# First sweep of a two-layer graph network: quads of slots instead of pairs on TensorE and ScalarE, gathered rows copied two quads ahead

## The reference, cut to what matters

```python
h = relu(layernorm(x))
x_l, x_r = h @ W_l + b_l, h @ W_r + b_r
e_emb = ea @ W_e                                    # ea: 64 features of each edge
m = leaky_relu(x_l[src] + x_r[dst] + e_emb, 0.2)
alpha = einsum('ehf,hf->eh', m, att)                # one score for each edge and head
ex = exp(alpha - segment_max(alpha, dst)[dst])
out = segment_sum(x_l[src] * (ex / denom[dst])[..., None], dst)   # self loops take part
x = x + relu(batchnorm(out.mean(heads) + bias))
```

## Time and profile before

| | before |
|---|---|
| median of three runs | 6867.18 us (6836.62 to 6873.22) |
| span of the profiled execution | 6810.8 us |
| PE busy | 4219.0 us |
| POOL busy | 3619.4 us |
| DVE busy | 3344.2 us |
| ACT busy | 1439.7 us |

### The profile page before, as it was taken

The page is one execution under the profiler, slowest core; times in us unless marked ns, Lnnn a source line. Parts: engine busy times, 40 slices in busy tenths (PEclk is TensorE's granted clock), DMA queues, the critical chain, the costliest instruction groups (busy, mean ns, idle before and its releaser), DMA issues. The chain is left out here.

```text
span 6810.8 us, 81310 instructions
## 1 busy us (share of the span) xinstructions
PE 4219.0 (62%) x16760; PEld 3105.7 (46%) x16761; DVE 3344.2 (49%) x8382; ACT 1439.7 (21%) x6145; POOL 3619.4 (53%) x3589
## 2 busy tenths in 40 slices
PE   4777777777777777768999998533333333333335
PEld 3555555555555555644444445333333333333335
DVE  6444444444444444479999998822222222222224
ACT  1111111111111111236666663400000000000000
POOL 2555555555555555305555551056666666666662
PEclk8888888888888888879999998755555555555555
DMA  6333333333333333324343441201111111111111
GB/s 106 92 93 95 93 93 94 95 99 95 96 93 93 98 92 93 98 81 124 110 111 109 110 112 50 57 20 23 23 23 23 23 23 23 23 23 23 23 23 28
DMA packets 609795, 478.35 MB, mean 70 GB/s; under 512 B 424696, under 2 KB 438034, under 8 KB 609334
## 3 DMA queue, kind: packets, MB, share of 16 engines
q1 hardware_dynamic: 440940, 256.05, 14.3%
q0 software_dynamic: 101184, 104.41, 7.2%
q10 hardware_dynamic: 67465, 115.81, 4.7%
HBM read 348.37 MB, written 126.73 MB: 70 GB/s over the span
## 5 line engine op out<-in xcount | busy, mean ns | idle before, releaser
L1417 POOL DMA_INDIRECT BR<-h2D,mS x1564 | 1476.9, 944 | 1007.4 <-issue 451.5
L585 POOL DMA_INDIRECT BR<-hD,AL x1308 | 1247.2, 953 | 1018.4 <-ACT ZR L634 638.4
L1441 PE MATMUL PS<-BR,ZR 128*128 x3328 | 796.1, 426 | 1507.1 <-DVE ZR L544 1086.3
L616 PE MATMUL PS<-Wz,BR 128*128 128x264 f32 x3328 | 1209.0, 449 | 696.3 <-DVE alq L682 319.0
L1441 PEld LDWEIGHTS PS<-BR,ZR 128*128 128x128 f32 x3328 | 735.9, 328 | 1567.3 <-issue 1563.9
L679 DVE SCALAR_TENSOR_TENSOR PS<-PS,a 128x528 f32<-128x528 f32 x832 | 594.8, 715 | 1543.4 <-PE PS L617 653.6
L1460 DVE TENSOR_TENSOR BR<-BR,PS 128x64 f32 x1664 | 362.6, 218 | 1725.3 <-remote 1306.5
L617 PE MATMUL PS<-BR 128*128 x3328 | 1150.8, 431 | 0.0
L940 PE MATMUL PS<-BR,ZR 128*128 128x329 f32 x3328 | 1027.9, 469 | 27.0 <-POOL BR L926 21.0
L616 PEld LDWEIGHTS PS<-Wz,BR 128*128 128x128 f32 x3328 | 653.9, 219 | 839.0 <-issue 587.1
L926 POOL TENSOR_TENSOR BR<-ZR,BR 128x768 f32<-128x768 f32 x416 | 616.1, 1481 | 416.6 <-ACT BR L912 414.7
(11 more groups left out here) (254 smaller groups left out, 2641.4 us busy)
## 6 DMA issues: line engine op xcount, KB each, us to landing
zD<-ZR ACTq DMA_DIRECT2D x416, 256.0 KB
ZR<-zD SPq DMA_DIRECT2D x416, 256.0 KB, 2.7
BR<-relD SPq DMA_DIRECT2D x105, 512.0 KB
ZR<-ea SPq DMA_DIRECT2D x1664, 32.0 KB
BR<-h2D,mS POOLq DMA_INDIRECT x1564
BR<-hD,AL POOLq DMA_INDIRECT x1308
AL<-hD SPq DMA_DIRECT2D x28, 224.0 KB, 2.6
BR<-hD,lmS POOLq DMA_INDIRECT x256
```

The lines of the kernel that those rows point to most:

```text
L585: Q.indirect_dma_start(HT[:, (t % G) * F:(t % G) * F + F], None, hD, bass.IndirectOffsetOnAxis(at_src, 0)).then_inc(hs[q % 16], 16)
L616: P.matmul(m, zo1[:, p % 2, (j % 2) * 128:(j % 2) * 128 + 128], Wz, start=True, stop=False)
L1417: Q.indirect_dma_start(BIG[:, j * F:j * F + F], None, h2D, bass.IndirectOffsetOnAxis(mS[:, (j // 16) % 4, j % 16:j % 16 + 1], 0)).then_inc ...
L1441: ins = P.matmul(bank3(j // 4)[:, j % 4, :], oh[:, (j // 4) % 4, j % 4, :], rows, start=True, stop=True)
```

## The change

In the first sweep, TensorE turns four slots into one whole PSUM bank and signals once; ScalarE copies 512 columns at once and signals once; TensorE takes that once for the two pairs of products. The quad q+1 is turned before the products of quad q. ScalarE copies the gathered rows of quad q+2 while it handles quad q, and two quads ahead of the loop. Its order for a quad is: copy of the turned quad, the register load where it is due, four row copies, the store. `zo1` becomes two buffers of 512 columns, of which the second lies beyond the old end of the tensor. To make room, `Wzs` (weights that are needed only after the sweeps) moves into the big tensor, is stored to DRAM before the sweep and loaded again after it. The register tables `ringD` and `needD` are shifted by the added quad.

```diff
-    BR = sb("BR", [128, 26000 + NS * 4 + 16 * AC])
+    BR = sb("BR", [128, 26000 + NS * 4 + 16 * AC + MC])
-    Wzs = sb("Wzs", [128, MC])
+    Wzs = BR[:, 26000 + NS * 4 + 16 * AC:26000 + NS * 4 + 16 * AC + MC]
-    zo1 = Rf[:, 1408:1920].rearrange("p (t c) -> p t c", c=256)
+    zo1 = Rf[:, 1408:1920], BR[:, 26000 + NS * 4 + 4992:26000 + NS * 4 + 5504]
+    wzsD = dram("wzsD", [128, MC])
...
+    dWs = dsem()
+    sv.wait(S)
+    dma(S, wzsD, Wzs, dWs)
...
+    dWs.wait(A)
...
-            def turn(p):
-                for j in (2 * p, 2 * p + 1):
-                    if j % 4 == 0:
-                        hc.take(P)
-                        es[(j // 4) % 8].take(P, 64)
-                    ins = P.transpose(PS[:, p % 2, (j % 2) * 128:(j % 2) * 128 + 128],
-                                      zring[:, j % 32, :, :].rearrange("p t f -> p (t f)"), ident)
+            def turn(q):
+                hc.take(P)
+                es[q % 8].take(P, 64)
+                for k in range(4):
+                    ins = P.transpose(PS[:, q % 2, k * 128:k * 128 + 128],
+                                      zring[:, (4 * q + k) % 32, :, :].rearrange("p t f -> p (t f)"), ident)
                 ins.then_inc(t_rdy.s, 1)
...
-                zo_rdy.take(P)
+                if p % 2 == 0:
+                    zo_rdy.take(P)
...
             turn(0)
-            for p in range(32):
-                if p + 1 < 32:
-                    turn(p + 1)
-                products(p)
+            for q in range(16):
+                if q + 1 < 16:
+                    turn(q + 1)
+                products(2 * q)
+                products(2 * q + 1)
...
+        def rows_of_quad(q, regs):
+            gf.take(A)
+            A.wait_ge(landed, regs[1])
+            for k in range(4):
+                ins = source_row(regs[0][k], 4 * q + k)
+                if k == 0:
+                    ins.then_inc(hf.s, 1)
+            ins.then_inc(hc.s, 1)
...
-            for p in range(32):
-                q = p // 2
+            for q in range(16):
                 t_rdy.take(A)
-                A.copy(zo1[:, p % 2, :], PS[:, p % 2, 0:256]).then_inc(zo_rdy.s, 1)
-                if not (last and q == 15):
-                    if p % 8 == 0:
...
+                A.copy(zo1[q % 2], PS[:, q % 2, :]).then_inc(zo_rdy.s, 1)
+                if q < n:
+                    if q % 4 == 0:
+                        k = 8 if last and q == 12 else 16
+                        A.load(offs[0:k], ringD[0:1, ds(i * 64 + 4 * q + 16, k)])
+                    rows_of_quad(q + 2, (offs[4 * (q % 4):4 * (q % 4) + 4], A.snap(needs[q], min_val=1, max_val=NG3 // 4)))
+                A.dma_start(zD[ds(i * 16 + q, 1), :, :].rearrange("a p c -> (a p) c"),
...
+    dma(S, Wzs, wzsD, dWs)
...
+    dWs.wait(P)
     turn_loops(0)
```

More of the change, by code:

```diff
@@ L280, in build @@
             dma(S, tabD[r, :].rearrange("(k p) -> p k", p=128), t, dB)
-        dma(S, ringD[0, 12:12 + NS].rearrange("(k p) -> p k", p=128), tI3, dB)
-        for o in (0, NQ1 + 15):
+        dma(S, ringD[0, 8:8 + NS].rearrange("(k p) -> p k", p=128), tI3, dB)
+        for o in (0, NQ1 + 14):
             dma(S, needD[0, o:o + NQ1].rearrange("(k p) -> p k", p=32), tN[3:128:4, :], dB)
@@ L615, in products @@
                     m = scores_of(p)[:, j % 2, :]
-                    P.matmul(m, zo1[:, p % 2, (j % 2) * 128:(j % 2) * 128 + 128], Wz, start=True, stop=False)
+                    P.matmul(m, zo1[(j // 4) % 2][:, (j % 4) * 128:(j % 4) * 128 + 128], Wz, start=True, stop=False)
                     ins = P.matmul(m, ohT[:, (j // 4) % 2, j % 4, :], xr, start=False, stop=True)
@@ L634, in source_row @@
             return A.copy(zring[:, slot % 32, 0, :], HT[:, ds(at_row, F)])
+        def rows_of_quad(q, regs):
[6 more added lines that the diff above has]
+            ins.then_inc(hc.s, 1)
         def some(i, last):
-            n = 15 if last else 16
+            n = 14 if last else 16
             A.load(needs[0:n], needD[0:1, ds(i * 16 + NQ1 + 16, n)])
-            for p in range(32):
-                q = p // 2
+            for q in range(16):
@@ L641, in some @@
                 t_rdy.take(A)
-                A.copy(zo1[:, p % 2, :], PS[:, p % 2, 0:256]).then_inc(zo_rdy.s, 1)
-                if not (last and q == 15):
-                    if p % 8 == 0:
[L645 to L659, removed]
-            close(t_rdy, gf)
[L662 to L668, removed]
@@ L669, in keep_turned @@
-        ins.then_inc(hc.s, 1)
+                A.copy(zo1[q % 2], PS[:, q % 2, :]).then_inc(zo_rdy.s, 1)
[5 more added lines that the diff above has]
+                A.dma_start(zD[ds(i * 16 + q, 1), :, :].rearrange("a p c -> (a p) c"),
+                            zring[:, 4 * (q % 8):4 * (q % 8) + 4, :, :].rearrange("p s t f -> p (s t f)")
+                            ).then_inc(st[q % 8].s, 16)
@@ L670, in keep_turned @@
+            close(t_rdy, gf)
+        A.load(needs[0:2], needD[0:1, NQ1 + 14:NQ1 + 16])
+        A.load(offs[0:8], ringD[0:1, 8:16])
+        for q in range(2):
+            rows_of_quad(q, (offs[4 * q:4 * q + 4], A.snap(needs[q], min_val=1, max_val=NG3 // 4)))
         close(gf)
```

## The result

The changed kernel takes 6931.91 us (6918.9 to 6936.63, four runs). The kernel before took 6870.2 us beside it on the same chip (6836.62 to 6882.61, four runs). The ratio is 1.0097, with a 95% interval of 1.0069 to 1.0125: the change makes the kernel 0.97% **slower**, and the forecast of 6806 us had the wrong sign. The profiled execution of after has a span of 6935.3 us against 6810.8, 124.5 us more. That is twice the 61.7 us between the medians: before's profiled execution was a fast one, so every difference between these two traces overstates the measured loss.

A forecast was written before the change was run, and what follows sets the result against it. Taken as bound: the sweep's relay of gather bursts and held PE signals. Cycle 27.15 against 27.78 us gives -62, start +4, end -3: -61 us, so 6806 us; range 6640 to 7010, the forecast's own 6735 to 6850.

The forecast's parts named there:

- The relay: First sweep: GpSimd bursts until tokens run out, then held PE signals arrive and ScalarE gives tokens; 27.8 us per four quads.
- Step (a): After the register load's token a burst starts; PE's signals are held until 11.56 us after the burst's start.
- (b): After the hold one turned quad is waiting, so the next gather comes 0.99 us later.
- (c): PE, stopped with full score buffers, needs 7.4 us to its next signal; a burst of four follows, without a hold.
- (d): Two pairs, then the quad with the register load, complete the four-quad cycle: 7.2 us.
- The copy of 512 columns: ScalarE's larger copy takes 0.54 us; saves 0.20 us a quad nobody waits for, puts 0.17 us more before the token.
- `Wzs`: Storing 135 KB to DRAM and loading it during the softmax is hidden: 0; uncovered, below 3.6 us.
- The 56 us carried over: The profile's span lies 56 us below the median of the runs; this was kept as an offset in the forecast time.
- The store as a beginning of the hold: In the first sweep, the hold of PE's signals begins after ScalarE's store in the middle of a gather burst.
- Rival one: A quad of slack really covers ScalarE's register load: 3.6 us a cycle leave the path, -352 us, 6515; chance 0.12.
- rival three: No difference: the sweep keeps two bursts of eight with a register load in one, -15 us, 6850; chance 0.20.
- Rival two: Slower because SyncE comes late with its loads during bursts: 2.6 us a cycle, +193 us, 7060; chance 0.26.

The follow-up runs named there:

- the pause: Changed kernel, but GpSimd waits after each quad of gathers until that quad has landed: 6796.24 us, 0.9927 of the kernel before, on a chip with holds.
- The early load: Changed kernel with ScalarE's register load moved behind the last store of the four-quad group: 6684.7 us with holds (0.9757 of before), 5545.07 without (1.0013).
- quads alone: Changed kernel with row copies one quad ahead instead of two: 6792.84 us with holds (0.9916 of before), 5779.61 without (1.0439).
- both runs without stores: ScalarE's first-sweep stores of `zD` left out: of the changed kernel 6875.6 us (1.0030 of before), of the kernel before 6904.64 us (1.0070).
- quads, one ahead, early load: Changed kernel with rows one quad ahead and the register load behind the group's last store: 6651.12 us with holds (0.9717 of before), 5547.77 without (1.0019).
- The early load with pairs: Kernel before with only the register load moved behind the group's last store: 5804.19 and 5800.02 us without holds (1.0459 and 1.0473 of before).

## Why the prediction was wrong

*What bounds the kernel: right in the main, for the chips with holds.* The relay, with signals of PE held during bursts, is what the sweep waits for there. On a chip without holds the same program's sweep takes 1956 instead of 2808 us, 852 less. For the changed kernel it is 2940 - 1971 = 969 us. The difference, 117 us, is nearly all of the sweep's loss of 132; by the medians of whole kernels it is 46 of 62 us. No run removes the holds alone, and the pause removes them at a price of its own.

*Step (a) failed.* It said that after the register load a burst of eight starts, and that the signals are held until 11.56 us after the burst's start, as in the cycle before. Its first half held: two tokens follow the load within 1.4 us. But the third quad's signal didn't wait until 11.56. At the loop's start PE has turned that quad early (tokens at 1340.05, 1341.41, 1343.47); in the other cycles the signal passed inside the burst or just behind it, at 8.5 to 10 us. Its token let the gathers go on, to twelve in one burst in 67 of 89 cycles, and so the hold went on until 17.0 to 17.2 us after the start: 5.5 us more than in (a). The prediction had written itself that PE now stands a quad further ahead of ScalarE, but it counted one burst of eight and one hold where three quads pass within 15 to 16 us.

The early load takes the pile behind the load away, and the load's own time in the token's path with it: 247 us. With one quad of rows ahead, where less can pile up, the same edit is worth 142 us (6793 to 6651). With pairs it was not measured on a chip with holds.

*Steps (b) to (d).* (b) is right: 1.00 us from the held copy to the gather (1357.64 to 1358.64) against 0.99. Of (c) and (d), 7.4 + 7.2 = 14.6 us, the cycle keeps 11.2 in the mean, since three quads have passed by then. In sum a cycle takes 29.2 us where I had 27.15 (ends of 25.2 and 29.0, just missed): 2.1 x 97.75 = 200 us, a little more than the miss in the profiled time (6935.3 against 6750, 185 us). That is a mean of unlike cycles, though. The prediction had all of them alike and gave the loop's end no term: the cycle across it takes 33.5 us, the other three 25.9, 28.4 and 28.9. Before, all lie between 27.1 and 28.6.

*Small terms.* The copy of 512 columns takes 0.585 us, not 0.54. It costs nothing that shows in sum: quads alone gained. Of `Wzs` nothing shows behind the sweep, where after is 9 us shorter. Signals and start were not measured apart.

*The 56 us carried over* were no offset. After's span, 6935.3 us, lies 3 us above its median, and the span of every other recorded run is 1.3 us below its time. The profiled execution of before was merely a fast one, below all 36 timed runs of that kernel on chips with holds (the fastest took 6816 us).

*The store as a beginning of the hold* is refuted by both runs without stores.

*Rival one* (load covered, 6515) and *rival three* (no difference) did not come on this chip; on the chips without holds the result is rival three's, for another reason. *Rival two* had the right sign and the wrong mechanism: SP ended 94 us of the row copies' idle time, less than before. SyncE's loads are slower during bursts, but nobody waited longer for them than before. They are not slower by a factor of two, as the prediction read: its 4.18 us are the first eight loads of a group, and a whole group of sixteen takes 11.63 us with no gather about, against 16.70 (lines at the end). The prediction gave the true case, slower through longer holds, no chance of its own: its test for a slower case asked only who is late for a token, not what happens when tokens come too close together.

## What to carry to other kernels

Where one engine's burst delays the signals of others, count how many tokens can be given in one burst, and look first at any long instruction that stands between the step that frees the producer and the step that gives the token: work piles up behind it. More lookahead can then be a loss: with quads it cost 139 us where signals are held and saved 226 us where they are not (5780 to 5554); with pairs it cost 41 us on the first kind and nothing on the other. Measure such a change on more than one chip before it is kept: of the variants, "quads, one ahead, early load" is 2.8% faster where signals are held and within 0.2% where they are not, and so is the one to keep. Quads alone are a gain of 0.8% or a loss of 4.4% by the chip. The early load with pairs loses 4.6 to 4.7% where none is held; with holds it wasn't measured. And look at the end of a loop as at a cycle of its own: a mean over all cycles hides it.

## What the runs showed of the hardware

- Chips differ. The same program took 6845 to 6870 us on three occasions and 5538 to 5551 us on three other chips, with equal instruction times (gather 0.95 and 0.96 us, L679 0.715 and 0.717 us). What differs is that PE's signals arrive late during gathers on the first kind: some 200 held pairs in the sweep against none. The granted clock differs too, 0.86 and 0.98, and so does the part behind the sweep, 3832 against 3436 us. Where no gather runs the kinds are alike: in 800 us of the second sweep PE does 2563 matmuls on the one (3200 to 4000 us) and 2567 on the other (2300 to 3100). In the last sweep, which gathers again, VectorE's L1460 has 740 us of "remote" between 5400 and 6700 us on the first kind, and none between 4200 and 5500 on the other. What makes a chip of one kind or the other isn't known.
- Most held signals are let through near the burst's end: in before's trace 1.69 us (median of 174) behind bursts of eight. A long burst lets some through in its midst: of some 140 held pairs of after's bursts of twelve, half were taken up 2.3 us (median) behind the burst's end, the other half before it, 60 of them over 4 us before.
- SyncE's issue depends on the kind of chip as well. Sixteen loads of edge rows took 16.70 us during bursts on the first kind, and 18.58 us in the cycle of after shown above. Behind the last gather they took 11.63 us there, and 11.61 us amid unbroken gathers on a chip without holds (after, then before, then before on the other chip):

```profile
1334.01 18.58 SPq L578 DMA_DIRECT2D ZR<-ea  x16
```

```profile
2943.90 11.63 SPq L573 DMA_DIRECT2D ZR<-ea  x16
```

```profile
1150.65 11.61 SPq L573 DMA_DIRECT2D ZR<-ea  x16
```

The Trainium skill, "DMA: Bandwidth & Descriptors", section "Issuing engines are not separate DMA queues", says that DMAs of several engines interleave, and that starting them on several engines saves only the sequencers' time. It doesn't say that one engine's issuing slows another's. The trace of the chip without holds agrees with that: gathers add nothing to SyncE's sixteen loads (11.61 against 11.63 us). On the first kind they add some 5 us.
